# First-layer start of a two-layer graph kernel on one core: x in groups of two tiles between W0's slabs, and the bias by matmul for four tiles only

## The chip, the core and the metric

The kernel runs on one core of a Trainium2 chip. The metric is the device time of one execution in microseconds (us), lower is better. Engines: TensorE (PE), VectorE (DVE), ScalarE (ACT), GpSimd (POOL) and SyncE (SP), which issues all DMAs here.

## What is computed

Two graph layers over 3327 nodes with 512 features; `adj` is 3327 x 3327 with 0 and 1. The change touches the start of the first layer.

```python
h = jnp.maximum(_layernorm(x, axis=-1), 0.0)
# layer 0
hidden = h @ W0 + b0
A = (adj != 0)
x = x + (A @ hidden) / A.sum(axis=0)[:, None]
# layer 1: layernorm and relu of x again, then attention with four heads
e = leaky_relu(src[:, :, None] + dst[:, None, :], 0.01) + adj[None]
x = x + (softmax(e) @ (h @ W1 per head)).mean(over heads)
```

## The kernel before

The nodes are 26 tiles of 128 (NT = 26; the last has 127 valid rows). Every engine runs a list of instructions in the order in which the program is written, and semaphores hold it where data are needed; there is no scheduler.

fp32 products are made from fp16 halves: a value is split in a high half (`_hi`, a rounding copy on ACT) and a low half (`_lo`, the rest, on DVE), and PE adds three products, high by high, high by low and low by high. This is done with W0 (`w0_high`, `w0_lo`, four slabs of 128 rows, scaled by a factor from the largest value of W0 and b0), with each transposed tile and with the hidden result.

One tile t goes through these steps in the first layer's start:

- SP loads x in groups (`load_x`, `groups0`), W0's four slabs and b0 broadcast to all partitions.
- DVE: `stats0(t)`; per group `variances0`, then, after a square root on ACT (`group0`), `scalars0`, six small operations.
- ACT: `relu0(t)`, which normalises and applies relu with the group's scalars.
- PE: `transpose0(t)`, four 128 x 128 transposes into one of two PSUM banks.
- ACT: `transposed_hi(t)`; DVE: `transposed_lo(t)`. Their results (`ht0`) have three places.
- PE: `hidden(t)`, 12 matmuls of 512 columns and one more that adds the bias: `b0_one`, a constant matrix, times `b0_16`, whose upper partitions hold b0's high half and lower ones its low half. The result goes to one of two PSUM banks.
- ACT: `hidden_hi(t)`; DVE: `hidden_lo(t)`, into `hid16`, from where the adjacency products read.

W0's scale: `w0_maximum` for each slab as it lands, `b0_maximum`, then a reduce to `w0mx`, a tiny matmul with ones on PE (L1331) that brings every partition's value together, and `w0_scale`.

After the start each of DVE, ACT and PE goes on in a loop over steps i. On DVE a step holds statistics of one or two coming tiles (two up to tile 19, then one), a group's variances and scalars where its last statistic is due, then `transposed_lo(i-2)` and `hidden_lo(i-4)`. On ACT it holds `relu0(i)`, `transposed_hi(i-2)`, `hidden_hi(i-4)`. On PE: `transpose0(t)`, then `hidden(t-2)`. From i = 26 on DVE also makes the first adjacency steps (`awork`, which turns a loaded pair of adjacency tiles into fp16 and keeps a maximum). PE then goes through 7 column blocks of 13 adjacency pairs (`pair`, L1351); the first block has 8 matmuls to a pair and needs `hid16` of its two tiles.

In the tiles' names of the profile `h_reg` holds x and h, `w_reg` W0, `ht0` and b0's halves, `row_reg` b0, `e_reg` `hid16`, `o_ps` and `c_ps` the PSUM banks.

## Time and profile before

| | us |
|---|---|
| median of 3 runs | 2495.39 |
| lowest and highest | 2494.52, 2496.39 |
| the profiled execution's own time | 2494.08 |
| its span, first to last instruction | 2492.3 |
| PE busy | 2447.1 (98%) |
| DVE busy | 1866.4 (75%) |
| ACT busy | 1258.9 (51%) |

The span lies 1.8 us under the execution's own time. A row of the timeline names start, duration, engine, line of the kernel, operation and tiles; `x4` merges four in a row. The chain of work that ended last is followed back from the last instruction: at each piece, to what released it. The first layer's start is the first 107 us of the 2492.

### The profile page before, as it was taken

Reading aid. Unit: us, or ns where it says so; the run is one execution under the profiler, and the core shown is the slowest. Engines: PE = TensorE matmul, PEld = TensorE weight load, DVE = VectorE, ACT = ScalarE, POOL = GpSimd, SP = SyncE. Lnnn points to the kernel's source line nnn. Section 1 sums busy time; section 2 is a strip of 40 time slices with the busy share of each in tenths; the row PEclk is TensorE's granted clock in tenths of the full one; section 3 lists DMA queues with packets and bytes.
Section 4 is the critical chain, followed back from the end, with each engine's and each line's share of the span. In section 5 each row is a group of like instructions: output and inputs, shape, how many; then the busy total and the mean of one; then the engine's idle time right before and its main releaser. Section 6 shows DMA issues by size and latency. Waiting matters only on the chain.

```text
span 2492.3 us, 42728 instructions
## 1 busy us (share of the span) xinstructions
PE 2447.1 (98%) x12328; PEld 1198.3 (48%) x12328; DVE 1866.4 (75%) x2560; ACT 1258.9 (51%) x1883; POOL 49.3 (2%) x44
## 2 busy tenths in 40 slices
PE   6999999799999999999999999999999999999999
PEld 3544447344444444444444444444444444444787
DVE  7588767876688766877668776687766887667776
ACT  4545546744455444554445544455444554444554
POOL 0000000000000000000000000000000000000000
PEclk9999999899999999999999999999999999999999
DMA  4286646200030000300003000030000300001000
GB/s 148 69 290 195 227 156 217 82 5 5 25 97 34 4 4 25 97 34 4 4 25 97 34 4 4 25 97 34 4 4 25 97 34 2 2 13 49 26 1 9
DMA packets 74223, 144.21 MB, mean 58 GB/s; under 512 B 4489, under 2 KB 11915, under 8 KB 72970
## 3 DMA queue, kind: packets, MB, share of 16 engines
q1 hardware_dynamic: 74122, 143.08, 17.5%
q8 instruction: 37, 0.61, 0.1%
q14 instruction: 64, 0.52, 0.1%
HBM read 129.37 MB, written 13.70 MB: 57 GB/s over the span
## 4 chain that ended last, share of the span: by engine, by line
PE 94%; DVE 3%; DMA 1%; issue 1%; ACT 1%; SPq 0%; DVEq 0%; ACTq 0%
PE z_ps L731 70%; PE o_ps L759 11%; PE o_ps L1351 3%; PE z_ps L1351 3%; PE z_ps L1404 2%; PE c_ps L1322 1%; PE o_ps L1322 1%; DMA ring_reg<-adjT_in 1%; PE c_ps L1351 1%; DVE hl_reg L917 1%; PE c_ps L1383 1%; PE o_ps L1375 0%; PE o_ps L1309 0%; DMA h_reg<-x_in 0%; DVE w_reg L952 0%
## 5 line engine op out<-in xcount | busy, mean ns | idle before, releaser
L731 PE MATMUL z_ps<-hl_reg,h_reg 128*128 (+2 forms) x8736 | 1759.0, 364 | 11.1 <-DVE hl_reg L608 11.1
L731 PEld LDWEIGHTS z_ps<-hl_reg,h_reg 128*128 (+1 forms) x8736 | 855.2, 98 | 911.4 <-DVE hl_reg L608 11.4
L559 ACT ACTIVATE hl_reg<-t_reg (+2 forms) x364 | 361.9, 994 | 731.5 <-DVE t_reg L635 379.4
L608 DVE TENSOR_TENSOR hl_reg<-t_reg,hl_reg (+2 forms) x364 | 417.6, 1147 | 235.0 <-ACT hl_reg L559 233.3
L544 ACT ACTIVATE t_reg<-ring_reg,vv 128x512 f32 (+3 forms) x728 | 526.3, 770 | 66.0 <-DVE ao_reg L623 60.3
L635 DVE SCALAR_TENSOR_TENSOR t_reg<-t_reg,vv,e_reg (+3 forms) x728 | 510.3, 743 | 7.7 <-issue 7.7
L623 DVE TENSOR_TENSOR ao_reg<-ao_reg,t_reg 128x1024 f32<-128x1024 f32 (+1 forms) x336 | 383.7, 1142 | 0.0
L759 PE MATMUL o_ps<-w_reg,z_reg 128*128 128x512 f16 x1248 | 278.2, 379 | 0.9 <-DVE z_reg L651 0.9
L759 PEld LDWEIGHTS o_ps<-w_reg,z_reg 128*128 128x128 f16 x1248 | 119.8, 98 | 140.9 <-DVE z_reg L651 1.2
L651 DVE SCALAR_TENSOR_TENSOR z_reg<-z_ps,z_reg 128x512 f16<-128x512 f32 (+1 forms) x112 | 73.2, 653 | 151.6 <-ACT z_reg L571 151.6
L456 ACT ACTIVATE e_reg<-e_reg (+2 forms) x91 | 90.1, 996 | 152.0 <-DVE e_reg L467 151.9
L467 DVE TENSOR_TENSOR e_reg<-e_reg,row_reg 128x512 f32 (+3 forms) x182 | 109.7, 647 | 0.0
L679 DVE SCALAR_TENSOR_TENSOR ao_reg<-o_ps,rcoef,ao_reg 128x512 f32<-128x512 f32 x104 | 75.8, 747 | 43.4 <-PE o_ps L759 40.6
L917 DVE TENSOR_TENSOR hl_reg<-hl_reg,ring_reg 128x1024 f32<-128x1024 f32 (+1 forms) x84 | 96.0, 1142 | 0.0
L571 ACT ACTIVATE z_reg<-z_ps 128x512 f16<-128x512 f32 (+1 forms) x112 | 63.4, 566 | 62.2 <-PE z_ps L731 60.9
L519 POOL TENSOR_TENSOR ao_reg<-ao_reg 128x512 f32<-128x512 f32 (+1 forms) x28 | 44.1, 1576 | 1978.6 <-DVE ao_reg L623 1978.6
L1192 ACT ACTIVATE ao_reg<-t_reg 128x512 f16<-128x512 f16 (+1 forms) x90 | 52.3, 583 | 56.5 <-DVE t_reg L908 56.4
L1351 PE MATMUL z_ps<-e_reg,t_reg 128*128 128x512 f16 x288 | 63.1, 379 | 0.0
L664 DVE RECIPROCAL rinv<-c_ps 128x4 f32<-128x4 f32 (+1 forms) x28 | 5.1, 181 | 66.5 <-PE c_ps L745 66.5
L1192 ACT ACTIVATE ao_reg<-hl_reg 128x512 f16<-128x512 f16 (+1 forms) x56 | 33.1, 594 | 38.1 <-DVE hl_reg L908 38.0
L1351 PE MATMUL o_ps<-e_reg,t_reg 128*128 128x512 f16 x216 | 49.6, 379 | 0.0
L908 DVE TENSOR_SCALAR t_reg<-ring_reg 128x1024 f16<-128x1024 f32 (+1 forms) x45 | 28.9, 642 | 21.3 <-DMA ring_reg<-adjT_in 11.8
(165 smaller groups left out, 1066.9 us busy)
## 6 DMA issues: line engine op xcount, KB each, us to landing
ring_reg<-adjT_in SPq DMA_DIRECT2D x78, 512.0 KB, 4.6
e_reg<-adjT_in SPq DMA_DIRECT2D x78, 512.0 KB, 3.6
ring_reg<-x_in SPq DMA_DIRECT2D x13, 512.0 KB, 4.2
x_dram<-ring_reg SPq DMA_DIRECT2D x13, 512.0 KB, 5.1
ring_reg<-c_dram SPq DMA_DIRECT2D x24, 256.0 KB, 3.3
ao_reg<-x_dram SPq DMA_DIRECT2D x6, 1024.0 KB, 5.6
out_dram<-ao_reg SPq DMA_DIRECT2D x6, 1024.0 KB, 4.4
h_reg<-x_in SPq DMA_DIRECT2D x3, 1536.0 KB, 16.7
```

What stands on the lines that cost most here:

```text
L456: nc.scalar.activation(e, e, ACT.Exp).then_inc(e_ready, 1)
L467: nc.vector.tensor_tensor(e, e, max_bc[:, 0:W], ALU.subtract).then_inc(e_sub, 1)
L544: nc.scalar.activation(t_ring[:, g % T_RING, u, 0:W], c_bc[:, h, 0:W], ACT.Relu, bias=vv4[:, 2, h, bass.ds(p * 2 + u, 1)], scale=vv4[:, 1, ...
L559: nc.scalar.activation(hl_ring[:, g % HL_RING, 0, :, 0:W], t_ring[:, g % T_RING, :, 0:W], ACT.Copy).then_inc(hi_ready, 1)
L608: nc.vector.tensor_tensor(hl_ring[:, g % HL_RING, 1, :, 0:W], t_ring[:, g % T_RING, :, 0:W], hl_ring[:, g % HL_RING, 0, :, 0:W], ALU.subtr ...
L623: nc.vector.tensor_tensor(acc, acc, tp, ALU.add).then_inc(acc_done, 1)
L635: nc.vector.scalar_tensor_tensor(out=tu, in0=tu, scalar=vv4[:, 0, h, bass.ds(p * 2 + u, 1)], in1=e_blk[:, bass.ds(p * 2 + u, 1), 0:W] .rea ...
L731: mm = nc.tensor.matmul(z_ps[:, k, 0:W], hk[hs], hl_ring[:, r, ps, u, 0:W], start=first and u == 0 and n == 0, stop=last and u == 1 and n ...
L759: mm = nc.tensor.matmul(o_ps[:, it % 3], z16[:, zs, k, it * P:(it + 1) * P], w16[:, k, h, ws], start=k == 0 and m == 0, stop=k == KT - 1 a ...
L917: nc.vector.tensor_tensor(acc, acc, adj_ring[:, s, :, 0:W], ALU.max).then_inc(adj_done, 1)
L1192: nc.scalar.activation(junk[:, u, 0:Wv], a_ring[a_slot[g]][:, u, 0:Wv], ACT.Copy, accum_out=degp3[:, 2 * p + u, n:n + 1]).then_inc(a_act, 1)
L1351: mm = nc.tensor.matmul(acc0(n, it), a[:, u, it * P:(it + 1) * P], hid16[:, 2 * p + u, s], start=p == 0 and u == 0 and s == 0, stop=p == P ...
```

## The change

Seven things change, all in the first 107 us:

- x's first two groups are tiles 0 and 1, and tiles 2 and 3 (before: 0, and 1 to 3). SP issues x group 0, W0's slabs 0 and 1, x group 1, slabs 2 and 3, then b0.
- The bias matmul stays for tiles 0 to 3 (`BIAS_PE = 4`). From tile 4 on DVE's new `hidden_sum(t)` reads the PSUM bank, scales it and adds b0 in fp32 into one of three places of `hid32`; `hidden_hi` and `hidden_lo` read these. PE's bank comes free with `hidden_sum` there. The last tile's mask is one more operation in `hidden_sum`.
- b0 in row form is scaled for that once, in step 6 (`b0_scale`); for the matmul's b0 its halves are made with the scale inside (`b0_lo`).
- DVE's and ACT's start is written in another order: statistics of tiles 0 to 3 between W0's maxima, both first transposed tiles before W0's low slabs; statistics from tile 4 on behind those slabs.
- In the loop, DVE does `transposed_lo` and the hidden operations ahead of statistics, and `scalars0` one step after `variances0`; ACT does `transposed_hi` and `hidden_hi` ahead of `relu0` and `group0`.
- Statistics come one step earlier (`stats_at`).
- PE transposes tiles 0 and 1 before `hidden(0)`, tile 2 before `hidden(1)`, tile 3 before tile 4.

```diff
-        groups0 = [(0, 1), (1, 4), (4, 8), (8, 14), (14, 20), (20, NT)]
+        groups0 = [(0, 2), (2, 4), (4, 8), (8, 14), (14, 20), (20, NT)]
+        BIAS_PE = 4
...
-            return 3 + (t - 4) // 2 if t < 20 else t - 9
+            return 2 + (t - 4) // 2 if t < 20 else t - 10
...
                 load_x(0)
-                for k in range(KT):
-                    sp.dma_start(w0_raw[:, k * D:(k + 1) * D], W0[k * P:(k + 1) * P, :]).then_inc(w0_in[k], 16)
+                load_w0(0)
+                load_w0(1)
+                load_x(1)
+                load_w0(2)
+                load_w0(3)
                 sp.dma_start(b0_bc, b0.partition_broadcast(P)).then_inc(b0_in, 16)
...
+                def b0_lo():
+                    dve.wait_ge(s_b0hi, 1)
+                    nc.vector.scalar_tensor_tensor(out=b0_16[P // 2:P], in0=b0_bc[P // 2:P], scalar=w0sc[P // 2:P],
+                                                   in1=b0_16[P // 2:P], op0=ALU.mult,
+                                                   op1=ALU.subtract).then_inc(s_b0lo, 1)
+                    nc.vector.tensor_scalar(w0coef[:], w0max[:], COEF0, None, ALU.mult)
...
+                    dve.wait_ge(s_b0lo, 1)
+                    link(dve, nc.vector.tensor_scalar(b0_bc, b0_bc, w0sc[:], SH * HS, ALU.mult, ALU.mult))
...
+                def hidden_sum(t):
+                    dve.wait_ge(hid_ps, t + 1)
+                    if t >= BIAS_PE + 3:
+                        dve.wait_ge(hid_lo, t - 2)
+                    h = hid32[:, t % 3]
+                    ins = nc.vector.scalar_tensor_tensor(out=h, in0=o_ps[:, 2] if t % 2 == 0 else c_ps[:], scalar=SH,
+                                                         in1=b0_bc, op0=ALU.mult, op1=ALU.add)
+                    if t == NT - 1:
+                        link(dve, ins)
+                        ins = nc.vector.tensor_scalar(h, h, valid[:, t:t + 1], None, ALU.mult)
+                    ins.then_inc(hid_sum, 1)
...
+                    if t < BIAS_PE:
+                        nc.vector.scalar_tensor_tensor(out=hid16[:, t, 1], in0=o_ps[:, 2] if t % 2 == 0 else c_ps[:],
+                                                       scalar=SH, in1=hid16[:, t, 0], op0=ALU.mult,
+                                                       op1=ALU.subtract).then_inc(hid_lo, 1)
+                    else:
+                        nc.vector.tensor_tensor(hid16[:, t, 1], hid32[:, t % 3], hid16[:, t, 0],
+                                                ALU.subtract).then_inc(hid_lo, 1)
...
-                for i in range(3, NT + 6):
+                for i in range(2, NT + 6):
+                    if 2 <= i - 2 < NT:
+                        transposed_lo(i - 2)
+                    if 0 <= i - 4 < BIAS_PE:
+                        hidden_lo(i - 4)
+                    if BIAS_PE <= i - 4 < NT:
+                        hidden_sum(i - 4)
+                    if BIAS_PE <= i - 5 < NT:
+                        hidden_lo(i - 5)
+                    for c in range(2, NG0):
+                        if i == group_at(c) + 1:
+                            scalars0(c)
                     for t in range(4, NT):
                         if i == stats_at(t):
                             stats0(t)
                     for c in range(2, NG0):
                         if i == group_at(c):
                             variances0(c)
-                            scalars0(c)
-                    if 1 <= i - 2 < NT:
-                        transposed_lo(i - 2)
-                    if 0 <= i - 4 < NT:
-                        hidden_lo(i - 4)
+                    if i == 6:
+                        b0_scale()
...
+                        act.wait_ge(hid_sum, t - BIAS_PE + 1)
+                        nc.scalar.activation(hid16[:, t, 0], hid32[:, t % 3], ACT.Copy).then_inc(hid_hi, 1)
...
-                    if t >= 2:
+                    if 2 <= t < BIAS_PE + 2:
                         pe.wait_ge(hid_lo, t - 1)
+                    elif t >= BIAS_PE + 2:
+                        pe.wait_ge(hid_sum, t - 1 - BIAS_PE)
```

Three places in the engines' orders. The first is ACT in the loop, at the root of the group of tiles 14 to 19, in the kernel before (`w_reg<-o_ps` is transposed_hi, `e_reg<-` hidden_hi, `h_reg<-` relu, `sd<-ve` the root):

```order
L1173 ACTIVATE w_reg<-o_ps 128x512 [waits hid_ps,tp_ps]
L1180 ACTIVATE e_reg<-c_ps 128x512 [waits hid_ps]
L237 ACTIVATE sd<-ve 128x6 [waits s_var]
L1166 ACTIVATE h_reg<-h_reg,nb,rs 128x512
L1173 ACTIVATE w_reg<-o_ps 128x512 [waits hid_ps,tp_ps]
L1180 ACTIVATE e_reg<-o_ps 128x512 [waits hid_ps]
```

and the same place now:

```order
L1202 ACTIVATE w_reg<-o_ps 128x512 [waits hid_ps,tp_ps]
L1212 ACTIVATE e_reg<-w_reg 128x512 [waits hid_sum]
L1195 ACTIVATE h_reg<-h_reg,nb,rs 128x512
L237 ACTIVATE sd<-ve 128x6 [waits s_var]
L1202 ACTIVATE w_reg<-o_ps 128x512 [waits hid_ps,tp_ps]
L1212 ACTIVATE e_reg<-w_reg 128x512 [waits hid_sum]
```

Hidden_hi reads SBUF (`w_reg`) and waits for `hid_sum`, which DVE raises; transposed_hi stands ahead of it as before, and the root now stands between relu and the next transposed_hi.

The second is DVE in the loop, in the kernel before, around the statistics of tiles 16 to 19 (`bst` is a statistic, `w_reg<-o_ps` transposed_lo, `e_reg<-` hidden_lo, `ve` a group's variance):

```order
L1005 TENSOR_TENSOR w_reg<-o_ps,w_reg 128x512 [waits ht_hi]
L1012 SCALAR_TENSOR_TENSOR e_reg<-o_ps,e_reg 128x512 [waits hid_hi]
L993 BN_STATS bst<-h_reg 128x6 x2
L1005 TENSOR_TENSOR w_reg<-o_ps,w_reg 128x512 [waits ht_hi]
L1012 SCALAR_TENSOR_TENSOR e_reg<-c_ps,e_reg 128x512 [waits hid_hi]
L993 BN_STATS bst<-h_reg 128x6 x2
L218 BN_AGGR mv<-bst 128x2 [waits s_bst]
L218 BN_AGGR mv<-bst 128x2 x5
L220 TENSOR_SCALAR ve<-mv 128x6 [waits s_mv]
L226 RECIPROCAL y<-sd 128x6 [waits s_sqrt]
```
and now:

```order
L1013 TENSOR_TENSOR w_reg<-o_ps,w_reg 128x512 [waits ht_hi]
L1021 SCALAR_TENSOR_TENSOR w_reg<-c_ps,row_reg 128x512 [waits hid_ps]
L1035 TENSOR_TENSOR e_reg<-w_reg,e_reg 128x512 [waits hid_hi]
L1001 BN_STATS bst<-h_reg 128x6 x2
L218 BN_AGGR mv<-bst 128x2 [waits s_bst]
L218 BN_AGGR mv<-bst 128x2 x5
L220 TENSOR_SCALAR ve<-mv 128x6 [waits s_mv]
L1013 TENSOR_TENSOR w_reg<-o_ps,w_reg 128x512 [waits ht_hi]
L1021 SCALAR_TENSOR_TENSOR w_reg<-o_ps,row_reg 128x512 [waits hid_ps]
L1035 TENSOR_TENSOR e_reg<-w_reg,e_reg 128x512 [waits hid_hi]
L226 RECIPROCAL y<-sd 128x6 [waits s_sqrt]
```
The statistics stand behind the tile's operations, hidden_sum (L1021) is new between transposed_lo and hidden_lo, and the group's reciprocal and what follows come a step later.

The third is DVE's start in the kernel before, behind the maximum over W0 and b0 (L982 scales b0, L976 is w0_lo):

```order
L971 RECIPROCAL w0sc<-w0max 128x1
L972 TENSOR_SCALAR w0sc<-w0sc 128x1
L982 TENSOR_SCALAR row_reg<-row_reg,w0sc 128x512
L983 TENSOR_SCALAR w0coef<-w0max 128x1
L984 TENSOR_SCALAR last_sc<-valid 128x1
L986 TENSOR_TENSOR w_reg<-row_reg,w_reg 64x512
L1005 TENSOR_TENSOR w_reg<-o_ps,w_reg 128x512
L976 SCALAR_TENSOR_TENSOR w_reg<-w_reg,w0sc 128x512
L993 BN_STATS bst<-h_reg 128x6
L976 SCALAR_TENSOR_TENSOR w_reg<-w_reg,w0sc 128x512
L993 BN_STATS bst<-h_reg 128x6
L976 SCALAR_TENSOR_TENSOR w_reg<-w_reg,w0sc 128x512 x2
```
and now:

```order
L976 TENSOR_SCALAR w0max<-z_ps 128x1
L977 RECIPROCAL w0sc<-w0max 128x1
L978 TENSOR_SCALAR w0sc<-w0sc 128x1
L1013 TENSOR_TENSOR w_reg<-o_ps,w_reg 128x512
L982 SCALAR_TENSOR_TENSOR w_reg<-w_reg,w0sc 128x512 x4
L988 SCALAR_TENSOR_TENSOR w_reg<-row_reg,w0sc,w_reg 64x512
L991 TENSOR_SCALAR w0coef<-w0max 128x1
L1001 BN_STATS bst<-h_reg 128x6 x4
L218 BN_AGGR mv<-bst 128x2 x4
L220 TENSOR_SCALAR ve<-mv 128x4
L1013 TENSOR_TENSOR w_reg<-o_ps,w_reg 128x512
L1031 SCALAR_TENSOR_TENSOR e_reg<-o_ps,e_reg 128x512
```
Four statistics now stand in a row behind all low halves, ahead of transposed_lo(2).

## Rows read from the trace of the kernel before

**Rows 1.** The page, part 4: the chain that ended last, by engine

```profile
PE 94%; DVE 3%; DMA 1%; issue 1%; ACT 1%; SPq 0%; DVEq 0%; ACTq 0%
```

**Rows 2.** Waits of PE: engine, line, waited-for; us in total, times, longest

```profile
PE o_ps L1309 <- ACT h_reg L1166: 10.0, 2, 8.4
```

**Rows 3.** Critical chain, 0 to 120 us: start us, us, what

```profile
30.09 0.63 PE o_ps L1309 x4
...
33.43 0.22 PE o_ps L1326
33.65 0.44 PE o_ps L1309 x4
34.09 2.59 PE c_ps L1322 x12
```

**Rows 4.** Timeline, 88 to 125 us

```profile
89.30 0.81 ACT L1166 ACTIVATE h_reg<-h_reg,nb,rs 128x512 f32<-128x512 f32 x1
...
90.01 0.59 ACT L1173 ACTIVATE w_reg<-o_ps 128x512 f16<-128x512 f32 x1
90.62 0.69 DVE L1005 TENSOR_TENSOR w_reg<-o_ps,w_reg 128x512 f16<-128x512 f32 x1 [0.50 <-ACT w_reg L1173]
...
107.19 10.52 PE L1351 MATMUL z_ps<-e_reg,t_reg 128*128 128x512 f16 x48
```

**Rows 5.** Timeline, 0 to 45 us: start us, us, engine, line, operation, tiles [idle]

```profile
3.52 0.69 DVE L993 BATCH_NORM_STATS2 bst<-h_reg 128x6 f32<-128x512 f32 x1 [2.44 <-DMA h_reg<-x_in]
...
4.16 0.69 DVE L958 TENSOR_REDUCE w0m<-w_reg 128x1 f32<-128x512 f32 x1
...
8.43 1.09 PE L1309 MATMUL o_ps<-ident,h_reg 128*128 128x128 f32 x4 [8.43 <-ACT h_reg L1166]
9.46 0.69 DVE L963 TENSOR_REDUCE w0m<-row_reg 128x1 f32<-128x512 f32 x1 [0.84 <-DMA row_reg<-b_in]
...
10.39 0.58 PE L1331 MATMUL z_ps<-w0mx,hl_reg 128*128 128x1 f32 x2 [0.88 <-DVE w0mx L966]
11.71 0.69 DVE L993 BATCH_NORM_STATS2 bst<-h_reg 128x6 f32<-128x512 f32 x1 [1.37 <-DMA h_reg<-x_in]
...
13.94 2.54 ACT L1212 ACTIVATE w_reg<-w_reg,w0sc 128x512 f16<-128x512 f32 x4
...
21.20 2.22 ACT L1166 ACTIVATE h_reg<-h_reg,nb,rs 128x512 f32<-128x512 f32 x3 [1.23 <-DVE nb L232]
...
22.07 1.36 PE L1309 MATMUL o_ps<-ident,h_reg 128*128 128x128 f32 x8 [1.55 <-ACT h_reg L1166]
...
36.52 0.51 DVE L218 BATCH_NORM_AGGREGATE mv<-bst 128x2 f32<-128x6 f32 x6
...
37.27 0.21 ACT L237 ACTIVATE sd<-ve 128x6 f32<-128x6 f32 x1 [2.99 <-DVE ve L220]
...
37.52 0.19 DVE L226 RECIPROCAL y<-sd 128x6 f32<-128x6 f32 x1 [0.27 <-ACT sd L237]
...
38.70 0.69 DVE L1005 TENSOR_TENSOR w_reg<-o_ps,w_reg 128x512 f16<-128x512 f32 x1
...
39.31 0.68 DVE L1012 SCALAR_TENSOR_TENSOR e_reg<-c_ps,e_reg 128x512 f16<-128x512 f32 x1
```

**Rows 6.** Busy time by stretch: stretch, length, busy by engine, PEclk, DMA share, GB/s

```profile
7.00:8.00 1.00, 0.00 (x0) 0.00 (x0) 0.93 (x5) 0.53 (x1) 0.00 (x0) 1.00 0.47 113
30.00:40.00 10.00, 9.91 (x52) 5.27 (x53) 9.49 (x27) 5.88 (x12) 0.00 (x0) 1.00 0.00 0
50.00:60.00 10.00, 10.00 (x55) 5.42 (x54) 6.19 (x11) 5.62 (x10) 0.00 (x0) 1.00 0.00 1
```

**Rows 7.** Groups by form, whole program, DVE and ACT: busy us, mean ns

```profile
L679 DVE SCALAR_TENSOR_TENSOR ao_reg<-o_ps,rcoef,ao_reg 128x512 f32<-128x512 f32 x104 | 75.8, 747 | 43.4 <-PE o_ps L759 40.6 <-DVE rcoef L666 0.8
...
L1012 DVE SCALAR_TENSOR_TENSOR e_reg<-o_ps,e_reg 128x512 f16<-128x512 f32 x13 | 8.9, 687 | 11.3 <-ACT e_reg L1180 11.3
...
L574 ACT ACTIVATE ao_reg<-ao_reg 128x512 f16<-128x512 f32 x24 | 14.9, 622 | 0.0
```

More of the change, by code:

```diff
@@ L158, in gnn_kernel @@
         w0m = sb("w0m", KT + 1, F32)
-        last_sc = sb("last_sc", 1, F32)
         wmx1 = sb("wmx1", 1, F32)
@@ L307, in gnn_kernel @@
         hid_ps = sem("hid_ps")
+        hid_sum = sem("hid_sum")
         hid_hi = sem("hid_hi")
@@ L1030, in _ @@
                 stats0(0)
+                stats0(1)
+                variances0(0)
                 w0_maximum(0)
[L1032 removed]
+                scalars0(0)
                 w0_maximum(1)
[L1034 removed]
+                stats0(2)
+                stats0(3)
                 w0_maximum(2)
+                variances0(1)
                 w0_maximum(3)
+                scalars0(1)
                 b0_maximum()
[L1038 removed]
+                transposed_lo(0)
                 w0_scale()
[L1040 to L1051 removed]
+                transposed_lo(1)
+                for k in range(KT):
+                    w0_lo(k)
+                b0_lo()
+                dve.wait_ge(s_const, 6)
+                for i in range(2, NT + 6):
[7 more added lines that the diff above has]
+                        hidden_lo(i - 5)
+                    for c in range(2, NG0):
+                        if i == group_at(c) + 1:
+                            scalars0(c)
                     for t in range(4, NT):
@@ L1176, in hidden_hi @@
                 def hidden_hi(t):
-                    act.wait_ge(hid_ps, t + 1)
-                    if t == NT - 1:
-                        act.wait_ge(s_lastsc, 1)
-                    nc.scalar.activation(hid16[:, t, 0], o_ps[:, 2] if t % 2 == 0 else c_ps[:], ACT.Copy,
-                                         scale=SH if t < NT - 1 else last_sc[:]).then_inc(hid_hi, 1)
+                    if t < BIAS_PE:
+                        act.wait_ge(hid_ps, t + 1)
+                        nc.scalar.activation(hid16[:, t, 0], o_ps[:, 2] if t % 2 == 0 else c_ps[:], ACT.Copy,
+                                             scale=SH).then_inc(hid_hi, 1)
+                    else:
+                        act.wait_ge(hid_sum, t - BIAS_PE + 1)
+                        nc.scalar.activation(hid16[:, t, 0], hid32[:, t % 3], ACT.Copy).then_inc(hid_hi, 1)
                 def degrees(g):
@@ L1216, in _ @@
                 relu0(0)
+                relu0(1)
                 transposed_hi(0)
-                act.wait_ge(s_b0sc, 1)
-                nc.scalar.activation(b0_16, b0_bc, ACT.Copy).then_inc(s_b0hi, 1)
+                transposed_hi(1)
+                group0(1)
+                relu0(2)
+                relu0(3)
                 for k in range(KT):
                     w0_high(k)
-                group0(1)
-                for i in range(1, NT + 5):
+                nc.scalar.activation(b0_16, b0_bc, ACT.Copy, scale=w0sc[:]).then_inc(s_b0hi, 1)
+                for i in range(3, NT + 5):
+                    if 2 <= i - 2 < NT:
+                        transposed_hi(i - 2)
+                    if 0 <= i - 4 < NT:
+                        hidden_hi(i - 4)
+                    if 4 <= i < NT:
+                        relu0(i)
                     for c in range(2, NG0):
@@ L1226, in _ @@
                             group0(c)
-                    if i < NT:
-                        relu0(i)
-                    if 1 <= i - 2 < NT:
-                        transposed_hi(i - 2)
-                    if 0 <= i - 4 < NT:
-                        hidden_hi(i - 4)
                 for g in range(NA):
@@ L1332, in _ @@
                 hidden(0)
-                for t in range(1, NT + 2):
+                transpose0(2)
+                hidden(1)
+                transpose0(3)
+                for t in range(4, NT + 2):
                     if t < NT:
                         transpose0(t)
-                    if t >= 3:
-                        hidden(t - 2)
+                    hidden(t - 2)
                 def pair(g):
```

45 lines of the change are left out of this document (12 added, 33 removed).

## The prediction

> **What bounds the kernel now.** I read the page's chain that ended last first: TensorE (PE) carries 94% of it [rows 1], so only two things shorten the kernel, less PE work or less waiting by PE. The list of whom PE waits for names 10.0 us for relu, in the first layer's start [rows 2]. Last, the chain up to 120 us [rows 3]. I number tiles t; T(t) is tile t's transposes, H(t) its hidden product. Up to T(4) at 30.09 us it changes between engines. From there it is PE alone, one piece after the other: H 2.59 us, bias matmul 0.22, T 0.44, so 3.25 us a tile, up to 107.19, where the adjacency stage's first matmul stands [rows 4]. Everything behind is PE with waits for things that themselves start from the end of H(25) or from adjacency matmuls. So what moves H(25)'s end moves the end of the kernel by as much. The question is when H(25) ends.
>
> **The bias matmul.** 22 of 26 go. Each is 0.22 us of PE in a stretch where nothing else is waited for [rows 3]: 22 x 0.216 = 4.8 us, if PE stays the bound. Instead DVE gets hidden_sum and ScalarE (ACT) waits for it.
>
> **The start.** The first x group is now 512 KB. Before, 256 KB landed at 3.5 us, and W0's first slab had landed by 4.16, since its maximum waited for nothing [rows 5]: for x's 512 KB I take 4.25. Up to b0's maximum DVE has 8 operations of 512 columns (0.60 us start to start, as 38.70 to 39.31 [rows 5]) and two groups of scalars. A group costs 1.18 us from its reciprocal on (37.52 to 38.70) and, with two tiles, 0.45 for aggregates and variance: 4.25 + 4.8 + 3.26 = 12.3. b0 is behind the same bytes as x's tiles 1 to 3 were before, and they had landed by 11.71 [rows 5]: b0 lands at some 11.7 and is covered by 0.6 us. Then as before: 0.93 us from b0's maximum to the matmul on all maxima and 0.6 for that [rows 5], three small operations of some 0.18 for the scale, so w0sc at 14.4; ACT makes four high slabs in 2.54 us, one every 0.61, and DVE low ones every 0.66, the first at 15.1, the fourth at 17.1, b0's at 17.8. PE has H(0) from 16.0 on, then T(2), H(1) and T(3), done by 22.6.
> But T(4) waits: DVE does four statistics (2.4 us, to 20.9), aggregates and variance (0.6), ACT the root, then transposed_hi(2) at 21.7; DVE transposed_lo(2) 22.3, hidden_lo(0) 22.9, scalars to 24.7. relu(4) starts at 24.76, and a T follows its relu's start by 0.87 us (21.20 to 22.07 [rows 5]): 25.6. PE has stood 3.1 us. H(2) starts at 26.1 against 30.7 [rows 3]: **4.6 us gained so far**.
>
> **Clock, a rule against the row.** PE now does nothing but two transposed tiles and one tiny matmul before H(0) at 16.0. What work after a rest costs stands in T(0)'s row: four transposes took 1.09 us at 8.43, and take 0.63 in T(4)'s [rows 3, 5], though the granted clock reads 1.00, the 2.4 GHz level, in each stretch [rows 6]. Some 2 us at half pace would end T(3) near 23.7 and stay inside the wait up to 25.6: I cost it at nothing. With that cover gone (all of H(0) and H(1) at half pace, 26 x 0.43 = 11.2, and T(2) and T(3) 0.9 each) T(4) would come at 28.9, 3.3 us late: that is the bound. The Trainium skill, "TensorE: Matmul & The Clock Gate", Part 1, says that the array's default is half rate and that activity has to release it; the 1.09 us agree with that, the granted clock shown doesn't. By that rule alone the 3.3 us would be lost only if all of the start stayed at half rate.
>
> **The rest of the layer, step by step.** PE alone would now go on at 3.25 up to T(6) and then at 2.59 + 0.44 = 3.03. Two others get in its way.
> First, DVE's list while it still makes two statistics a step. 0.60 for each 512-column operation; six aggregates and a variance 0.75 (36.52 to 37.27 [rows 5]) and 0.1 for the wait on the last statistic; scalars 1.18 + 0.07. Steps (i as in the loop) start with transposed_lo(i-2) at: i=6 28.5, i=7 33.1 (held by H(2)'s end, b0_scale and the root), i=8 36.7, i=9 39.8, i=10 44.4, i=11 48.0, i=12 51.2. That is 3.2 to 4.6 us a step with T(i) following 2.7 us behind: T(8) at 39.4 instead of 38.2, T(9) 42.5, T(10) 47.1, T(11) 50.7, T(12) 53.9. Five waits of PE, 1.2 + 0.1 + 1.6 + 0.6 + 0.1 = 3.5 us. Before, no such wait stands in the chain from T(4) on.
> Second, a ring that PE isn't part of. ACT's order is transposed_hi(i-2), hidden_hi(i-4), relu(i); hidden_hi now waits for hidden_sum(i-4), which stands on DVE behind transposed_lo(i-2), which waits for transposed_hi(i-2). So one step can't be shorter than: transposed_hi to transposed_lo 0.61 (90.01 to 90.62 [rows 4]), to hidden_sum 0.60, hidden_sum's own time and handoff 0.72, hidden_hi 0.53, relu 0.71 (89.30 to 90.01 [rows 4]) = **3.17 us**. Two terms have no row. hidden_sum: between 0.69 (the PSUM reader with a constant scalar) and 0.75 (with a scalar from memory [rows 7]); the scalar is a constant, so 0.69. hidden_hi now reads SBUF: the nearest row, an fp16 copy out of SBUF, is busy 0.62 [rows 7], and start to start ACT needs 0.1 less than the busy time (relu: 0.81 busy, 0.71): 0.53, with 0.48 (as out of PSUM) and 0.71 (as relu) as ends. That gives 3.12 to 3.41 a step. So from T(12) to T(25): 13 x 3.17 = 41.2, plus 0.85 once, where ACT waits for the last group's variances with transposed_hi behind it: T(25) at 95.9.
> Then 0.44 + 3 x 2.59 = 8.2, against 8.9 with bias: **H(25) ends at 104.1, against 107.2 [rows 4]: 3.1 us gained**. Of 4.6 + 4.8 = 9.3 us (less rounding), 3.5 + 13 x 0.14 + 0.85 = 6.2 are lost.
>
> **Edits at nothing.** Adjacency step 3 comes some 1 us later against H(25)'s end (hidden_sum(25), its mask and hidden_lo(24) stand ahead of it on DVE): its tile is ready some 2.6 us after the end, and PE wants it three pairs of 8 x 0.22 = 1.7 us later, 5.2. Without that cover it would be that 1 us. SP issues one DMA more, 0.43 us, ahead of b0; x's later groups are all there before 30, where no DMA moves any more [rows 6], and the statistics of tile 14 come at 35. last_sc is gone, b0_scale is counted above.
>
> **Rivals.** (A) PE stays the bound from T(4) on: neither the DVE steps nor the ring hold it. Speaks for it: DVE is busy 6.2 of 10 us from 50 on, ACT 5.6 [rows 6]. Against: the ring's terms are rows, and DVE has 9.5 of 10 us busy at 30 to 50 already [rows 6]. All 9.3 us: 2486.1. (B) The ring is longer than before's 3.25: with the upper ends, 3.41, four steps at the head and 13 after lose 17 x 0.24 = 4.1 us: 2496.4, slower than before. It decides from 3.35 us a step on. Against: the scalar is a constant. (C) b0 comes late. If the queue moved the 0.79 MB ahead of b0 at the slowest rate seen there, 113 GB/s at 7 to 8 us [rows 6], b0 would land at 16.4, 4.1 behind DVE: 2496.4 too; it costs from 12.3 on and turns the sign at 15.4. Against: b0's maximum began at 9.46 and x's 0.79 MB had landed at 11.71 [rows 5], 2.25 us for as many bytes. (D) The gain is had but not passed on, because a later wait ends by something fixed: the change would be worth nothing, 2495.4. Nothing behind depends on a time of day; all adjacency loads wait for DVE's steps.
>
> **How the numbers follow.** The sum is against the profiled execution's own 2494.08 us: 2491.0. The three runs have the median 2495.39, 1.3 above it, and lie 1.9 apart, so I forecast 2495.39 - 3.1 = 2492.3. A measurement tells some 0.2%, 5.0 us, from no change. Forecast 0.72 (own range 2490.0 to 2494.8, with 1 us for x's landing and the clock, 1 for the ring and 1 for the runs), A 0.12, B 0.08, C 0.05, D 0.03. Range 2488.0 to 2495.8. Faster by over 0.2% (below 2490.4): A and 0.1 of the forecast's lower end, 0.22. Slower by over 0.2% (above 2500.4): 0.03, as only B and C together or a cause I don't see reach it. Within: 0.75.
>
> **What would show it.** In after's timeline: T(4) at 25.6 with PE idle 3 us for relu; relu to relu 3.17 us and PE's idle 0.1 to 0.2 at each T between 54 and 95, put down to ACT's relu; larger ones at T(8) to T(11); the first adjacency matmul at 104.1. PE without idle there, and that matmul near 98, is A. A ring of 3.35 or more is B. DVE idle ahead of b0's maximum is C. The same start of the adjacency stage with another total would break the claim that all behind it only shifts.

## The result and the profile after

| | before | after |
|---|---|---|
| median of 20 runs each | 2495.34 | 2491.32 |
| lowest and highest | 2493.82, 2499.0 | 2489.41, 2493.2 |
| profiled execution's own time | 2494.08 | 2492.67 |
| its span | 2492.3 | 2491.0 |
| first adjacency matmul | 107.19 | 104.81 |

The ratio of the times is 0.9982, with a 95% interval of 0.9976 to 0.9988: 4.0 us less. The forecast was 2492.3, in a range of 2488.0 to 2495.8, most of the chance on "within 0.2%". That is what came. But the working was right for a part of the time only, and the 4.0 us are not the 2.4 by which the boundary (the first adjacency matmul) moved. Both have to be told. The changed kernel's runs, these 20 and 11 more made later, fall in two groups, 17 at 2489.4 to 2491.4 and 14 at 2492.2 to 2493.2 with none between, and both of its profiled executions are in the upper one.

The list of waits of the changed kernel, up to 110 us (us in total, times, longest), answers to [rows 2]:

```profile
ACT e_reg L1212 <- DVE w_reg L1021: 31.0, 21, 3.2
DVE w_reg L1013 <- ACT w_reg L1202: 18.0, 20, 1.3
PE o_ps L1343 <- ACT h_reg L1195: 13.2, 6, 8.9
```

The first two are the ring that the prediction spoke of: ACT's hidden_hi waits 21 times for DVE's hidden_sum, DVE's transposed_lo 20 times for ACT's transposed_hi. The third is what PE pays: 8.9 at T(0), where nothing can be had, and five waits more.

The timeline of the start (start us, us, engine, line, operation, tiles, idle before it), the answer to [rows 5]:

```profile
4.50 1.29 DVE L1001 BATCH_NORM_STATS2 bst<-h_reg 128x6 f32<-128x512 f32 x2 [3.42 <-DMA h_reg<-x_in]
...
12.68 0.68 DVE L969 TENSOR_REDUCE w0m<-row_reg 128x1 f32<-128x512 f32 x1
...
14.80 2.56 ACT L1243 ACTIVATE w_reg<-w_reg,w0sc 128x512 f16<-128x512 f32 x4 [0.49 <-DVE w0sc L978]
...
16.46 5.05 PE L1358 MATMUL o_ps<-w_reg 128*128 128x512 f16 x12 [2.27 <-DVE w_reg L982]
...
21.56 0.60 PE L1343 MATMUL o_ps<-ident,h_reg 128*128 128x128 f32 x4
22.00 2.75 PE L1358 MATMUL c_ps<-w_reg 128*128 128x512 f16 x12
...
24.80 0.60 PE L1343 MATMUL o_ps<-ident,h_reg 128*128 128x128 f32 x4
...
25.42 0.81 ACT L1195 ACTIVATE h_reg<-h_reg,nb,rs 128x512 f32<-128x512 f32 x1 [1.95 <-DVE nb L232]
...
26.29 0.66 PE L1343 MATMUL o_ps<-ident,h_reg 128*128 128x128 f32 x4 [0.88 <-ACT h_reg L1195]
...
26.78 2.75 PE L1358 MATMUL o_ps<-w_reg 128*128 128x512 f16 x12
...
40.07 0.66 PE L1343 MATMUL o_ps<-ident,h_reg 128*128 128x128 f32 x4 [1.03 <-ACT h_reg L1195]
```

H(0)'s twelve matmuls took 5.05 us, 0.43 apart, where H(1)'s took 2.75, 0.22 apart. T(4) still waited for relu, by 0.88. Then PE's rows from 46 us on, and at 105:

```profile
47.84 0.66 PE L1343 MATMUL o_ps<-ident,h_reg 128*128 128x128 f32 x4 [1.35 <-ACT h_reg L1195]
...
51.33 0.66 PE L1343 MATMUL o_ps<-ident,h_reg 128*128 128x128 f32 x4 [0.25 <-ACT h_reg L1195]
...
68.02 0.66 PE L1343 MATMUL o_ps<-ident,h_reg 128*128 128x128 f32 x4 [0.76 <-ACT h_reg L1195]
...
104.81 3.40 PE L1393 MATMUL z_ps<-e_reg,t_reg 128*128 128x512 f16 x15
```

And one turn of the ring, all engines, which answers to [rows 4]:

```profile
71.04 0.57 ACT L1202 ACTIVATE w_reg<-o_ps 128x512 f16<-128x512 f32 x1
...
71.65 0.69 DVE L1013 TENSOR_TENSOR w_reg<-o_ps,w_reg 128x512 f16<-128x512 f32 x1 [1.28 <-ACT w_reg L1202]
...
72.25 0.68 DVE L1021 SCALAR_TENSOR_TENSOR w_reg<-o_ps,row_reg 128x512 f32<-128x512 f32 x1
...
72.97 0.63 ACT L1212 ACTIVATE e_reg<-w_reg 128x512 f16<-128x512 f32 x1 [1.35 <-DVE w_reg L1021]
73.50 0.80 ACT L1195 ACTIVATE h_reg<-h_reg,nb,rs 128x512 f32<-128x512 f32 x1
74.21 0.57 ACT L1202 ACTIVATE w_reg<-o_ps 128x512 f16<-128x512 f32 x1
```

0.61 + 0.60 + 0.72 + 0.53 + 0.71 = 3.17 us from one transposed_hi to the next, each term as the prediction had it. Two stretches, in the columns of [rows 6]:

```profile
30.00:40.00 10.00, 9.04 (x47) 4.48 (x45) 8.75 (x25) 4.77 (x10) 0.00 (x0) 1.00 0.01 2
50.00:60.00 10.00, 9.75 (x51) 4.79 (x49) 7.96 (x14) 5.94 (x11) 0.00 (x0) 1.00 0.00 0
```

DVE went from 6.2 to 8.0 busy us of the 10 from 50 on, and PE, which was busy for all 10 before, now stands for 0.25.

### The profile page after: what moved, and what is told of

It is laid out like the page before. It is cut to its first block, busy times and chain, and to the rows that moved or that the text cites. A ratio compares the mean times of both kernels' runs of the same rounds, so it can differ in the third digit from the quotient of the medians.

```text
span 2491.0 us, 42724 instructions
## 1 busy us (share of the span) xinstructions
PE 2447.7 (98%) x12306; PEld 1196.4 (48%) x12306; DVE 1878.7 (75%) x2582; ACT 1260.4 (51%) x1883; POOL 49.4 (2%) x44
## 4 chain that ended last, share of the span: by engine, by line
PE 94%; DVE 4%; DMA 1%; ACT 1%; issue 1%; SPq 0%; DVEq 0%; ACTq 0%
PE z_ps L731 70%; PE o_ps L759 11%; PE o_ps L1393 3%; PE z_ps L1393 3%; PE z_ps L1446 2%; PE c_ps L1393 1%; PE o_ps L1358 1%; PE c_ps L1358 1%; DVE hl_reg L923 1%; PE c_ps L1425 1%; DMA ring_reg<-adjT_in 1%; PE o_ps L1417 1%; PE o_ps L1343 0%; DVE bst L1001 0%; DVE w_reg L958 0%
## 5 line engine op out<-in xcount | busy, mean ns | idle before, releaser
L731 PEld LDWEIGHTS z_ps<-hl_reg,h_reg 128*128 (+1 forms) x8736 | 855.3, 98 | 911.5 <-DVE hl_reg L608 11.4
L1393 PEld LDWEIGHTS z_ps<-e_reg,t_reg 128*128 128x128 f16 x288 | 28.2, 98 | 34.0
```

Source lines behind the costliest of these rows:

```text
L731: mm = nc.tensor.matmul(z_ps[:, k, 0:W], hk[hs], hl_ring[:, r, ps, u, 0:W], start=first and u == 0 and n == 0, stop=last and u == 1 and n ...
L1393: mm = nc.tensor.matmul(acc0(n, it), a[:, u, it * P:(it + 1) * P], hid16[:, 2 * p + u, s], start=p == 0 and u == 0 and s == 0, stop=p == P ...
```

## The experiments

Three marks of each profile say where time goes: the boundary; PE's transposes behind its 1.97-us wait at some 362 us; and those behind its next long wait (3.4 us), at some 438. From the third mark to the end of the span 13 of the 14 profiles take 2052.2 to 2052.9 us, and one (scalars and sum first) 2051.2. "Mark shift" is the second mark against the mean of before's two profiles, 366.75; "time shift" the median against that of before's runs made beside it, which was 2495.3 to 2496.9. "Before, again" is a single execution, of 2497.3 us.

| kernel | boundary | boundary to second mark | second to third | mark shift | time shift | median, ratio (95%) |
|---|---|---|---|---|---|---|
| before | 107.19 | 258.23 | 74.7 | | | |
| before, again | 107.92 | 260.16 | 74.7 | | | |
| after | 104.81 | 257.48 | 76.3 | -4.5 | -4.0 | 2491.3, 0.9976 to 0.9988 |
| after, again | 105.17 | 257.04 | 76.3 | -4.5 | -5.1 | 2491.2, 0.9973 to 0.9991 |
| sum first | 100.25 | 257.04 | 74.7 | -9.5 | -9.5 | 2486.6, 0.9951 to 0.9978 |
| bias kept | 103.30 | 258.24 | 74.7 | -5.2 | -4.1 | 2492.1, 0.9975 to 0.9993 |
| bias kept, again | 103.17 | 258.66 | 74.7 | -4.9 | -4.7 | 2492.2, 0.9974 to 0.9992 |
| bias part alone | 110.47 | 257.05 | 74.7 | +0.8 | -0.1 | 2496.0, 0.9991 to 1.0009 |
| bias part, sum first | 104.89 | 257.05 | 76.3 | -4.8 | -5.0 | 2490.8, 0.9969 to 0.9988 |
| large fillers | 116.17 | 257.05 | 74.7 | +6.5 | +6.0 | 2502.1, 1.0016 to 1.0039 |
| small fillers | 106.40 | 257.04 | 74.7 | -3.3 | -3.6 | 2492.3, 0.9975 to 0.9994 |
| scalars and sum first | 99.13 | 257.05 | 74.7 | -10.6 | -11.3 | 2484.5, 0.9941 to 0.9969 |
| the same, small fillers | 98.42 | 257.05 | 76.3 | -11.3 | -9.7 | 2486.1, 0.9943 to 0.9972 |
| scalars first alone | 104.42 | 257.04 | 74.7 | -5.3 | -5.1 | 2491.2, 0.9970 to 0.9988 |

The medians follow the second mark within 1.6 us, most within 0.8. They don't follow the boundary alone (before's mean 107.55): the kernels with the bias matmul kept gain 0.3 us or less beyond their boundary's shift, those without it 1.3 to 3 (0.6 where the third stretch is 76.3 and the boundary the earliest). What lies between is told at the end of this section.

**The ring, opened.** In the changed kernel's loop on DVE, hidden_sum goes ahead of transposed_lo:

```diff
                 for i in range(2, NT + 6):
+                    if BIAS_PE <= i - 4 < NT:
+                        hidden_sum(i - 4)
                     if 2 <= i - 2 < NT:
                         transposed_lo(i - 2)
...
-                    if BIAS_PE <= i - 4 < NT:
-                        hidden_sum(i - 4)
```

> The changed kernel with one swap on VectorE: hidden_sum(i-4) stands ahead of transposed_lo(i-2) in each step, so ScalarE's hidden_hi no longer waits behind transposed_lo. Ring theory: the ring of 3.17 us a tile is open, TensorE goes on at 2.59 + 0.44 = 3.03 us from tile 12 on, T(8) comes 0.6 us earlier, the 0.8 us at the last group's root goes, and the adjacency stage starts near 100.2 us instead of 104.8 (99.5 to 101.5); total 4.6 us below the changed kernel, 2486 to 2487.5. Rival (TensorE's idle gaps have another cause, the waits themselves or the PSUM banks): the pace stays at 3.17 and the stage starts at 104 to 105, total as the changed kernel.

The boundary came at 100.25, where the ring had it (100.2), and the median is 9.5 us under before's. The timeline of one turn, at the same place as above:

```profile
70.85 0.60 PE L1343 MATMUL o_ps<-ident,h_reg 128*128 128x128 f32 x4
71.05 0.69 DVE L1021 SCALAR_TENSOR_TENSOR w_reg<-c_ps,row_reg 128x512 f32<-128x512 f32 x1 [1.14 <-PE c_ps L1358]
...
71.66 0.68 DVE L1013 TENSOR_TENSOR w_reg<-o_ps,w_reg 128x512 f16<-128x512 f32 x1
71.78 0.63 ACT L1212 ACTIVATE e_reg<-w_reg 128x512 f16<-128x512 f32 x1 [1.21 <-DVE w_reg L1021]
...
73.88 0.38 PE L1343 MATMUL o_ps<-ident,h_reg 128*128 128x128 f32 x2
```

DVE's sum now waits for PE, not for ACT's work on another tile, and PE's transposes are 3.03 us apart, 2.59 + 0.44, its own work. The order of two instructions on DVE was worth 4.6 to 4.9 us at the boundary. The ring is shown.

**The bias matmul kept, all else as changed.**

```diff
-        BIAS_PE = 4
+        BIAS_PE = 25
```

> The changed kernel with the bias matmul back for tiles 4 to 24 (BIAS_PE = 25); only the last tile goes through hidden_sum. Ring theory: hidden_hi waits for TensorE alone again, no ring, TensorE goes at 3.25 us a tile with no gap from T(5) on, and the adjacency stage starts at 103.1 us (102.8 to 104), 1 to 2 us before the changed kernel's 104.8: the 21 matmuls less are worth less than nothing there. Rival (TensorE's work is the bound, each bias matmul counts): 21 x 0.216 = 4.5 us later, 109.3 us.

Boundary 103.30 (expected 103.1), 1.5 us before that of the changed kernel, though PE has 21 more matmuls of 0.22 us: no wait of PE stands between T(4) and the boundary, each tile 3.25 us. So up to the boundary the new order alone gives 3.9 us, and taking the bias matmul away gives 1.5 back to the ring and DVE's longer list. Yet the median is no worse than the changed kernel's (2492.1 and 2491.3 or 2491.2, intervals of some 2 us). That was my first sign that something behind the boundary depends on the bias matmul.

**The bias part alone, in the old order**: before, with the changed kernel's hidden_sum, hidden_hi and hidden_lo, b0's rows scaled in step 6, and the sum behind transposed_lo:

```diff
                     if 1 <= i - 2 < NT:
                         transposed_lo(i - 2)
-                    if 0 <= i - 4 < NT:
+                    if 0 <= i - 4 < BIAS_PE:
                         hidden_lo(i - 4)
+                    if BIAS_PE <= i - 4 < NT:
+                        hidden_sum(i - 4)
+                    if BIAS_PE <= i - 5 < NT:
+                        hidden_lo(i - 5)
+                    if i == 6:
+                        b0_rows()
```

> The kernel before with the bias part of the change alone: its own order, groups and loads, and hidden_sum for tiles 4 to 25. Ring theory: 3.17 us a tile at best instead of 3.25 (21 x 0.075 = 1.6 us), 0.65 at the end, and each of the three group steps, with statistics, variances and scalars ahead of transposed_lo in the ring, costs 1 to 2 us: adjacency stage at 106 to 109 us against 107.2 before, total within 2 us of before. Rival (each bias matmul counts): 107.2 - 22 x 0.216 = 102.4, total 4.8 us below before.

110.47, 2.6 to 3.3 us later than before's boundary and 1.5 outside what I expected. PE's timeline:

```profile
30.85 0.63 PE L1338 MATMUL o_ps<-ident,h_reg 128*128 128x128 f32 x4 [1.87 <-DVE w_reg L1008]
31.45 4.44 PE L1353 MATMUL o_ps<-w_reg 128*128 128x512 f16 x12
...
53.01 0.63 PE L1338 MATMUL o_ps<-ident,h_reg 128*128 128x128 f32 x4 [1.44 <-DVE w_reg L1008]
73.57 0.63 PE L1338 MATMUL o_ps<-ident,h_reg 128*128 128x128 f32 x4 [1.35 <-DVE w_reg L1008]
```

Up to 1.7 of it is H(2), 4.44 instead of 2.75, after a wait of 1.87; behind the same wait before's H(2) took 2.75 in both its profiles, so this much is the execution's. The waits of 1.44 and 1.35 come where a group's variances and scalars stand ahead of the hidden operations in one step. The median is before's, and the second mark comes only 0.8 later; why is told at the end of this section.

**The bias part, sum first**: the same kernel with hidden_sum ahead of transposed_lo.

```diff
+                    if BIAS_PE <= i - 4 < NT:
+                        hidden_sum(i - 4)
                     if 1 <= i - 2 < NT:
                         transposed_lo(i - 2)
...
-                    if BIAS_PE <= i - 4 < NT:
-                        hidden_sum(i - 4)
```

> The kernel before with the bias part alone, and hidden_sum ahead of transposed_lo on VectorE. Ring theory: with the ring open the 22 bias matmuls count in the old order as well, 3.03 us a tile from tile 4 on, less what the group steps cost: the adjacency stage at 102.4 to 104.5 us against 107.2 before and 110.5 with the ring, total 2.5 to 5 us below before. Rival (the old order's statistics ahead of the tile's work are what holds it, not the ring): 106 to 110.

Boundary 104.89, 5.6 us before that of the kernel with the sum behind, and a median 5.0 us under before's. Of the 5.6 us, 3.6 arise from T(10) on (57.5 us from there to the boundary with the sum behind, 53.9 now); the rest holds the other kernel's slow H(2) and its start, which was 0.3 later. The boundary is 0.4 past what I expected. H(1) took 3.94 instead of 2.75 here, but that cost nothing: T(4) followed T(3) by 5.30 us in both kernels. What was larger than I had allowed is what DVE's list cost PE: 66.2 us from T(4) to T(25) for 64.1 of PE's own work, 1.18 of it in a wait at T(10). So the bias part with its operations in this order is worth, as far as medians tell, as much as all seven parts together in the order that they have.

**Half pace in the start, tried with large fillers**: 15 fp32 matmuls of 512 columns around the maximum's matmul, into a bank that nobody reads.

```diff
+                for _ in range(12):
+                    nc.tensor.matmul(z_ps[:, 1], ident[:], xs[:, 0], start=True, stop=True)
                 pe.wait_ge(s_w0mx, 1)
                 nc.tensor.matmul(z_ps[:, 0, 0:1], ones_m, w0mx[:], start=True, stop=True).then_inc(w0b_ps, 1)
+                for _ in range(3):
+                    nc.tensor.matmul(z_ps[:, 1], ident[:], xs[:, 0], start=True, stop=True)
```

> The changed kernel with 15 matmuls more on TensorE, whose results nobody reads, between the first two tiles' transposes and H(0). Theory (the slow start of H(0), 12 matmuls 0.43 us apart, is covered by the wait for relu(4)): H(0) goes as fast as W0's low halves come and ends 1.5 to 2 us earlier, T(4) stays at 26.3 and the adjacency stage at 104.8 us, total within 0.5 us of the changed kernel. Rival (the slow start costs): T(4) and the stage come 1 to 2 us earlier.

The twelve took 11.75 us and pushed the maximum's matmul from 13.60 to 22.39: I had sized them wrongly, and the run says nothing of the clock's worth. It does say that the boundary's 11.4 us (116.17 against 104.81) arrive at the second mark as 10.9 and at the end as 10 to 11 (a time shift of 6.0 against -4.0 and -5.1), so hardly anything behind swallows a delay.

**Small fillers**: 20 fp16 matmuls of 128 columns on each side of the maximum's.

```diff
+                for _ in range(20):
+                    nc.tensor.matmul(z_ps[:, 1, 0:P], b0_one, b0_one, start=True, stop=True)
                 pe.wait_ge(s_w0mx, 1)
                 nc.tensor.matmul(z_ps[:, 0, 0:1], ones_m, w0mx[:], start=True, stop=True).then_inc(w0b_ps, 1)
+                for _ in range(20):
+                    nc.tensor.matmul(z_ps[:, 1, 0:P], b0_one, b0_one, start=True, stop=True)
```

> The changed kernel with 40 small fp16 matmuls of 128 columns more on TensorE, 20 on each side of the maximum's matmul, whose results nobody reads. Unlike the 15 fp32 matmuls of the run before (24 rows in 11.75 us, so the maximum itself came late) they fit into TensorE's rest. Theory (the slow start of H(0), matmuls 0.43 us apart, lies under the wait for relu(4)): H(0) and T(3) end 1 to 2 us earlier, T(4) stays at 26.3 us and the adjacency stage at 104.8, total as the changed kernel. Rival (the slow start costs): the stage comes 1 to 2 us earlier.

PE's timeline, and the busy time from 26 to 32 us with the granted clock 0.72 as its third number from the end:

```profile
16.36 2.75 PE L1358 MATMUL o_ps<-w_reg 128*128 128x512 f16 x12 [1.14 <-DVE w_reg L982]
...
26.19 0.66 PE L1343 MATMUL o_ps<-ident,h_reg 128*128 128x128 f32 x4 [3.08 <-ACT h_reg L1195]
26.69 4.44 PE L1358 MATMUL o_ps<-w_reg 128*128 128x512 f16 x12
```

```profile
26.00:32.00 6.00, 5.81 (x23) 2.81 (x24) 3.56 (x6) 2.91 (x7) 0.00 (x0) 0.72 0.28 87
```

H(0) ran at full pace and PE was done 2.3 us earlier. T(4) came at 26.19 instead of 26.29, since it waits for DVE and ACT: the half pace of H(0) had cost 0.1 us. But PE now rested 3.08 us instead of 0.88, the granted clock fell, and H(2) took 4.44: boundary 106.40, 1.6 us later than the changed kernel's, which neither the theory nor the rival had. A wait filled in one place had moved to another, where it cost more.

**The first scalars and the sum first**: the ring's cure, and in the step behind the first loop group its scalars ahead of everything, so that relu(4) doesn't wait behind two tiles' work.

```diff
                 for i in range(2, NT + 6):
+                    if i == group_at(2) + 1:
+                        scalars0(2)
+                    if BIAS_PE <= i - 4 < NT:
+                        hidden_sum(i - 4)
...
-                    if BIAS_PE <= i - 4 < NT:
-                        hidden_sum(i - 4)
...
-                        if i == group_at(c) + 1:
+                        if c > 2 and i == group_at(c) + 1:
```

> The kernel with hidden_sum ahead of transposed_lo, and in step 4 the scalars of tiles 4 to 7 ahead of VectorE's other work. Theory (T(4) waits for relu(4), which waits for VectorE's list): relu(4) starts 1.6 us earlier, at 24; T(4) then waits for TensorE's own slow H(0), H(1), T(3) and comes at 25.3 instead of 26.5; VectorE's list at tiles 8 to 11 keeps part of it, the adjacency stage starts at 99.3 to 99.9 instead of 100.25. Rival (T(4) isn't on the path that sets the stage, VectorE's list alone is): 100.2.

```profile
25.05 1.04 PE L1345 MATMUL o_ps<-ident,h_reg 128*128 128x128 f32 x8
...
38.62 0.65 PE L1345 MATMUL o_ps<-ident,h_reg 128*128 128x128 f32 x4 [0.44 <-ACT h_reg L1197]
...
48.49 0.66 PE L1345 MATMUL o_ps<-ident,h_reg 128*128 128x128 f32 x4 [0.51 <-ACT h_reg L1197]
...
99.13 10.52 PE L1395 MATMUL z_ps<-e_reg,t_reg 128*128 128x512 f16 x48
```

T(3) and T(4) now go back to back, and two waits of half a microsecond are all that PE has left up to the boundary, which came 0.2 before the expected 99.3 to 99.9. 2484.5 us, ratio 0.9955 (0.9941 to 0.9969): the fastest of all, 6.8 under the changed kernel.

**The same with the small fillers** of above.

> The kernel before it (scalars first) with the 40 small matmuls. Theory (with the wait for relu(4) short, the slow start of H(0) is no longer covered): T(4) at 24.7 instead of 25.3, the adjacency stage 0.3 to 0.6 us earlier than without the small matmuls, 98.9 to 99.4. Rival (the start's pace never matters): no difference between the two.

98.42, 0.7 before the kernel without fillers and 0.5 before what I expected: H(0) is short here, T(4) comes at 24.49 and waits 1.39 instead of 3.08, and H(2) kept its 2.75. So where the wait for relu(4) is short the slow start does cost, and the rival fell. In the medians of five runs each, 2486.1 and 2484.5, this gain is not seen; the profile with the fillers has the 76.3 in its third stretch.

**The changed kernel again, and the scalars first alone** (the diff above without the lines of the sum).

> The changed kernel once more, unchanged. Nothing of it hangs on a theory of the start: first adjacency matmul at 104.8 us again. It tells whether the stretch from the first wait for the second layer's norm (362.3) to the second (438.6), 76.3 us in the first profile against 74.7 in all others but one, belongs to the kernel (then 76.3 again) or to that one execution (then 74.7, and a span near 2489.4).

> The changed kernel with its own order of hidden_sum and transposed_lo, so with the ring, and only the scalars of tiles 4 to 7 ahead in step 4. Theory (start and ring are two separate prices): T(4) at 25.5 us, the ring's 3.17 us a tile stays, the adjacency stage at 103.6 (103.4 to 104.0). Rival (the ring takes the start's gain back): 104.5 to 104.8.

The third stretch of the changed kernel was 76.3 again. By what I had written ahead that makes it the kernel's, but this test was too weak: two profiles of other kernels have it too, the code there is the same in all, and 17 of the changed kernel's 31 runs are in its lower group, of which there is no profile. Whether it meets this kernel more often than others is open.

104.42 with the scalars first, 104.81 and 105.17 without, and all the ring's waits still in it: 1.04, 1.34, 0.25 and 0.76. That is 0.4 later than expected and 0.1 short of the rival's range, so the boundary by itself doesn't decide between them. T(4) does: it came at 25.96 here, 0.33 and 0.64 before the changed kernel's two, and the boundary 0.39 and 0.75 before theirs. What is gained in the start passes through the ring; it was only less than forecast. The two profiles of the changed kernel differ by 0.36 at the boundary, since H(0) took 5.28 in one and 5.05 in the other: T(2) behind it came 0.45 later, transposed_hi(2) 0.28, and T(4) 0.31. So the slow start isn't free even in the changed kernel; it reaches T(4) through T(2) and ACT, though PE still waits for relu(4) there.

**What depends on the bias matmul behind the boundary.** The profiles with the bias on PE are the only ones longer than 257.5 from the boundary to the second mark, two of two up to here. Two repeats ask about this alone:

> The kernel before once more, one execution. Its first profile waits 1.00 us at about 312 us for the row maximum (rows_mx), which makes its stretch from the first adjacency matmul to the 1.97-us wait 258.23 us long; nine of eleven profiles have 257.04 or 257.05. If that wait belongs to the bias matmul on TensorE (both profiles that have it fully, this kernel's and that of the kernel with the bias kept for tiles 0 to 24, have the bias there), the stretch is again 258.2 and the boundary near 107.2. If it is chance, as the 0.25 us in one of two profiles of the changed kernel suggests, it can be anything from 257.0 to 258.3; 257.1 or less refutes the first.

> The changed kernel with the bias matmul kept for tiles 0 to 24 once more. Boundary 103.3 again. Stretch behind it: 258.2 if the bias matmul is what makes the 1.0-us wait at rows_mx, anything from 257.0 if it is chance. Time: 2490.7 to 2492.3, if the first; some 1.2 us less at a stretch of 257.0, with a median that then follows how often the wait comes.

The stretches came at 260.16 and 258.66, both longer than the expected 258.2: the wait was there again with the bias, but its size is not fixed. Before's boundary came at 107.92 instead of near 107.2, since b0 landed later (its maximum began at 10.14 instead of 9.46).

The lists of PE's waits of the two (before again, then bias kept again):

```profile
PE o_ps L1351 <- DVE rows_mx L1020: 2.9, 1, 2.9
```

```profile
PE o_ps L1393 <- DVE rows_mx L1042: 1.4, 1, 1.4
```

With the bias on PE this wait is 1.00, 2.95, 1.02 and 1.44. In the ten profiles without, it is 0.25 once and otherwise not there. It can be followed back. DVE is late at the row maximum because the adjacency tiles that it waits for land late, behind each of the four slabs of W1's reload. DVE's row at the fourth, in before, in before again and in after:

```profile
289.26 0.69 DVE L908 TENSOR_SCALAR hl_reg<-ring_reg 128x1024 f16<-128x1024 f32 x1 [4.58 <-DMA ring_reg<-adjT_in]
```

```profile
291.94 0.69 DVE L908 TENSOR_SCALAR hl_reg<-ring_reg 128x1024 f16<-128x1024 f32 x1 [4.45 <-DMA ring_reg<-adjT_in]
```

```profile
286.14 0.69 DVE L914 TENSOR_SCALAR hl_reg<-ring_reg 128x1024 f16<-128x1024 f32 x1 [4.75 <-DMA ring_reg<-adjT_in]
```

Counted from the boundary (written + from here on) these are +182.07, +184.02 and +181.33, and the two kernels with the bias kept have +182.10 and +182.51. Take 181.07 from each and you have PE's five waits at the row maximum within 0.01: 1.00, 2.95, 0.26, 1.03, 1.44. The nine profiles without the wait have +180.2 to +180.7. So the wait hangs on when this load lands.

Two of the four reloads make the lateness. The first ends DVE's wait at +139.7 to +140.2 with the bias and +138.5 to +138.8 without, though the loads are issued at +132.31 and +132.71 in all. The third ends it 14.1 to 16.1 us behind the second with the bias and 13.8 to 14.4 without. The DMA view of the 9 us around the first in before and in after (queues; issues with median us to landing):

```profile
q8 instruction: 1, 0.02, 0.6%
issues: line engine op xcount, KB each, median us to landing
ring_reg<-adjT_in SPq DMA_DIRECT2D x4, 512.0 KB, 8.2
```

```profile
ring_reg<-adjT_in SPq DMA_DIRECT2D x4, 512.0 KB, 7.3
```

With the bias, a packet of the queue that loads instructions (q8) comes at +137, in the middle of the first reload's loads, which take 8.2 to 8.7 us to land. In nine of the ten profiles without, no packet is near (the changed kernel has them at +141 and at +169, the small fillers' kernels at +130 and +158), and the loads take 7.1 to 7.4. The tenth, with the large fillers, has one at +132.4, just ahead of the loads' issue, and they take 6.7. The packets come every 24 to 30 us here, and 22 matmuls fewer shift them against the boundary by some 4 to 7 us, out of the loads' way.

The third reload speaks less clearly. With the bias, a packet comes there at +161.9 to +162.8, behind the first load's issue, and the loads take 7.2, 8.7, 7.2 and 7.9 us; without, 7.2 to 7.7. So a packet among the loads does not always make them slow. The delay of the loads and the shift of the packets are shown, and so is their coincidence at the first reload; that the packet itself is what delays them, and how 0.02 MB can cost a microsecond, is an inference. A kernel with the bias matmul kept and other instructions in PE's stream, so that the packets miss the loads, would test it, and wasn't run.

## Why the prediction was right, and where it wasn't

- **x and b0.** The start was 0.25 late (4.50 against 4.25) and b0's maximum came at 12.68 against 12.3, with no wait for b0. Rival C fell. W0's high slabs began at 14.80, some 0.4 late, and H(0) at 16.46 against 16.0.
- **Clock.** I allowed 2 us at half pace; all of H(0) went so, 12 x 0.43, while the granted clock reads 1.00. T(3) ended at 25.4 instead of 23.7, and the cover (PE waits for relu(4)) held by 0.88 instead of 1.9, and that partly by luck: with T(4) at the forecast 25.6 it would have been 0.2. It cost almost nothing, as priced: small fillers took the half pace away and T(4) came 0.1 earlier. But in the changed kernel's second profile H(0) took 0.23 more and T(4) came 0.31 later through T(2), a path that I had not looked at. The Trainium skill ("TensorE: Matmul & The Clock Gate", Part 1: half rate until activity releases it) agrees with the 5.05 us of H(0) and with H(1) at full pace. My bound, all of H(0) and H(1) at half pace, did not come.
- **The start's gain.** T(4) at 26.29 against 25.6 and H(2) at 26.78 against 26.1: 3.9 gained, not 4.6. The missing 0.7 had gathered on DVE by the end of its four statistics (21.6 against 20.9), most of it from the delays of the first point, and it stays 0.6 to 0.7 to the end.
- **DVE's steps.** T(8) to T(12) at 40.07, 43.24, 47.84, 51.33 and 54.50, forecast 39.4, 42.5, 47.1, 50.7 and 53.9: right in spacing within 0.15. The rows show waits of 1.03, 1.35 and 0.25 only, as the rest lies in gaps too short for a row to show; by the spacing above 3.03 PE lost 1.18, 0.14, 1.57, 0.46 and 0.14, 3.5 in all. The five waits that I had listed add up to 3.6, not to the 3.5 that I wrote; the boundary doesn't hang on it.
- **The ring.** 3.17 a tile, each term right, and 0.76 for the last group's root against 0.85. Opening it gave PE its 3.03 back. Rivals A and B fell, and D with the large fillers' delay, which arrives at the end.
- **The boundary.** 104.81 against 104.1: 2.4 us gained of 3.1 forecast.
- **Behind the boundary: the step that failed.** I wrote that everything behind only shifts, and named the same boundary with another total as what would break that. It broke. The profiles of before have a wait for the row maximum of 1.00 and 2.95 us that the changed kernel has at 0.25 and not at all, 0.75 to 2.95 us of gain that no term held. I had counted that wait among the "waits for things that themselves start from the end of H(25) or from adjacency matmuls" and didn't ask whether its size depends on what lies beside its loads. The median's 3.1 forecast and 4.0 measured are near each other because a start 0.7 worse stands against this, which is luck. Why the loads beside it land later with the bias matmul stays open.
- **The two shown spans** differ by 1.3 only, since in both profiles of the changed kernel PE's clock fell at the second mark (below) and cost 1.6. That need not be the kernel's: its runs fall in two groups some 1.7 apart, which fits a loss that only some executions have, and the same loss came in two profiles of other kernels.

The bias matmul's removal is then two opposite things, read from the changed kernel's two profiles against the two with the bias kept: 1.5 to 2.0 us lost at the boundary, 0.8 to 1.6 won behind. In the changed kernel's order they cancel within what the medians can tell; with the sum first the loss goes, and the kernel gains some 5 us more. The 3.9 us of the other parts at the boundary were measured together; x's groups, the transposed tiles' place and the earlier statistics weren't tried apart.

## What to carry to other kernels

When work moves from the bounding engine to two others that hand tiles to each other, draw the chain that one step has in their orders: here two instructions of DVE in the other order were worth 4.6 us, more than the 22 matmuls' removal in the order as given. Filling a rest of an engine only helps if what it then waits for is earlier too; otherwise the rest moves. And compare a stretch far behind the change between two profiles of each kernel before calling it a mere shift.
